# Eight graphs a loop turn, root and scatter one step earlier, and a second home for the last column tile's rows

## What is computed

```python
# layer 0: x = LN(x + D^-1/2 (adj + I) D^-1/2 (x W) + bias)
# layer 1, with h the output of layer 0 and adj the edges' weights:
m_j = h @ W1[:D];  m_i = h @ W1[D:]
pre = m_j[:, None, :, :] + m_i[:, :, None, :] + b1       # [b, i, j, o]
msg = gelu(layernorm(pre, g1, be1))
agg = einsum('bijo,bij->bio', msg, adj)
upd = layernorm(concat([h, agg]) @ W2 + b2, g2, be2)
out = layernorm(h + upd)
```

## Time and profile before

| | us |
|---|---|
| median of 3 runs | 3649.75 (3649.69 to 3650.8) |
| the profiled execution | 3647.8 |
| its span, first to last instruction | 3646.1 |
| PE busy | 3232.9 (89%) |
| ACT busy | 3045.4 (84%) |
| DVE busy | 2937.8 (81%) |
| POOL busy | 2123.0 (58%) |
| DMA, both queues with data | 30% of 16 engines |

### The profile page before, as it was taken

How to read it: one execution, slowest core, us unless ns; L and a number is a source line. 1 busy time by engine, 2 the same in 40 slices (tenths; PEclk the granted TensorE clock), 3 DMA queues, 4 the chain that set the end, 5 groups by cost and what they waited for, 6 DMA issues and landing times.

```text
span 3646.1 us, 88379 instructions
## 1 busy us (share of the span) xinstructions
PE 3232.9 (89%) x26504; PEld 2974.1 (82%) x26505; DVE 2937.8 (81%) x6816; ACT 3045.4 (84%) x8038; POOL 2123.0 (58%) x2628
## 2 busy tenths in 40 slices
PE   4899988989889898889998899988999988989888
PEld 2788888888878888888888888888888888888887
DVE  3788888877878788888788887887887888878887
ACT  3888888988879888888888888888888888988887
POOL 4555666555655556655566655566555666555652
PEclk7999999999989999999999999999999999999999
DMA  2333323223323233332332323333323323223321
GB/s 83 100 95 111 103 94 119 93 86 105 112 80 96 89 102 102 108 110 80 102 103 91 121 78 96 101 105 108 103 87 102 103 92 121 85 89 103 104 91 47
DMA packets 284246, 355.71 MB, mean 98 GB/s; under 512 B 28208, under 2 KB 242736, under 8 KB 283696
## 3 DMA queue, kind: packets, MB, share of 16 engines
q1 hardware_dynamic: 250928, 231.55, 21.7%
q0 software_dynamic: 32768, 117.47, 8.5%
HBM read 223.09 MB, written 125.83 MB: 96 GB/s over the span
## 4 chain that ended last, share of the span: by engine, by line
PE 54%; DVE 17%; ACT 8%; POOL 8%; issue 7%; DMA 5%; DVEq 1%; ACTq 0%; SPq 0%; POOLq 0%; PEldq 0%
PE z_odd_ps L1362 9%; PE agg_odd_ps L1321 9%; PE agg_even_ps L1321 8%; PE z_even_ps L1362 7%; POOL table L512 7%; DMA table<-stage,row_id 5%; DVE pick L1076 4%; PE p_ps L1173 3%; DVE spread L1105 3%; PE z_odd_ps L1358 2%; DVE msg L1051 2%; PE z_even_ps L1358 2%; ACT root L656 2%; DVE stage L940 2%; PE p_ps L1165 2%
## 5 line engine op out<-in xcount | busy, mean ns | idle before, releaser
L711 ACT ACTIVATE tmp<-nbr,r_sb 128x128 f32<-128x128 f32 x4032 | 1262.4, 389 | 25.0
L512 POOL DMA_INDIRECT table<-stage,row_id x512 | 830.3, 1622 | 219.8 <-issue 189.4
L1076 DVE SCALAR_TENSOR_TENSOR pick<-rank,root_p 128x512 f32<-128x512 bf16 (+3 forms) x1536 | 821.3, 564 | 111.3 <-PE z_odd_ps L1362 53.5
L1105 DVE SCALAR_TENSOR_TENSOR spread<-nbr 128x512 f32<-128x512 bf16 (+3 forms) x1536 | 827.5, 564 | 6.9 <-PE agg_even_ps L1321 5.6
L696 ACT ACTIVATE msg<-msg 128x768 f32<-128x768 f32 x768 | 647.2, 843 | 46.2 <-issue 23.5
L1362 PEld LDWEIGHTS z_odd_ps<-mi_g,pick 128*128 128x128 f32 x4608 | 594.4, 200 | 28.8 <-issue 5.0
L1321 PE MATMUL agg_odd_ps<-spread,msg 128*128 128x128 f32 x4608 | 592.5, 280 | 27.3 <-issue 19.6
L1362 PE MATMUL z_odd_ps<-mi_g,pick 128*128 128x129 f32 x4608 | 602.3, 282 | 0.0
L1362 PEld LDWEIGHTS z_even_ps<-mi_g,pick 128*128 128x128 f32 x4608 | 569.1, 193 | 26.8 <-issue 1.9
L527 POOL COPY root_extra<-root_p 128x32 f32<-128x32 f32 (+4 forms) x768 | 276.5, 360 | 530.4 <-ACT root_p L670 530.4
L1321 PEld LDWEIGHTS agg_odd_ps<-spread,msg 128*128 128x128 f32 x4608 | 557.7, 196 | 30.1 <-issue 29.1
(11 more groups left out here) (219 smaller groups left out, 4663.2 us busy)
## 6 DMA issues: line engine op xcount, KB each, us to landing
nbr<-table SPq DMA_DIRECT2D x128, 640.0 KB, 4.8
adj_g<-in_adj SPq DMA_DIRECT2D x32, 1024.0 KB, 7.2
nbr_root<-table SPq DMA_DIRECT2D x128, 256.0 KB, 5.5
nbr_extra<-table SPq DMA_DIRECT2D x384, 70.0 KB
nbr_extra<-table SPq DMA_DIRECT2D x128, 90.0 KB
nbr_extra<-table SPq DMA_DIRECT2D x256, 40.0 KB
x_g<-in_x SPq DMA_DIRECT2D x32, 256.0 KB, 3.4
table<-stage,row_id POOLq DMA_INDIRECT x512, 6.2
```

Source lines behind the costliest of these rows:

```text
L512: pool.indirect_dma_start(table[q], bass.IndirectOffsetOnAxis(ap=row_id[:, jt * TB + it:jt * TB + it + 1], axis=0), stage[:, jt, it, :], N ...
L711: last = act.activation(tmp[:, c % 2, n - FROM[u], :], half_row, ACT.Identity, scale=r_sb[:, c % 2, n - FROM[u]:n - FROM[u] + 1])
L1076: ins = dve.scalar_tensor_tensor(into.rearrange("p k n -> p (k n)"), rank[:, it % 2, span], float(MARK + t), root_p[:, it % 2, span], ALU. ...
L1105: ins = dve.scalar_tensor_tensor(into, ranks(nbr[:, it, jt:jt + count, A_RANK:A_ROOT]), float(MARK + t), nbr[:, it, jt:jt + count, A_ADJ:A ...
```

## The change

`S_ROOT` and `S_SCATTER` go one step back, `S_XB` three steps on; the loop's turn has eight graphs, with four written out ahead of it and four behind; `half` is gone, the root's middle values lie in the rows where the root will stand, and `own` borrows `sqi`; the rows of column tile 3 have a second tensor that every other graph uses.

```diff
+ENDS, TURN_OF = 4, 8
-S_XT, S_DEG, S_XB, S_AT, S_EDGE = 0, 0, 1, 1, 4
+S_XT, S_DEG, S_XB, S_AT, S_EDGE = 0, 0, 4, 1, 4
-S_HB, S_MJ, S_MI, S_SEED, S_ROOT, S_SCATTER, S_OVER, S_OVERS = 18, 17, 21, 17, 19, 20, 22, 23
+S_HB, S_MJ, S_MI, S_SEED, S_ROOT, S_SCATTER, S_OVER, S_OVERS = 18, 17, 21, 17, 18, 19, 22, 23
...
-        half = sb("half", [P, TB, N])
-        stage = sb("stage", [P, TB, TB, ROW])
+        rows_sb = sb("rows_sb", [P, TB, TB, ROW])
+        last_rows = sb("last_rows", [P, TB, ROW])
+        def stage(q, jt):
+            return last_rows[:, :, :] if jt == TB - 1 and q else rows_sb[:, jt, :, :]
+        def halfway(q, jt):
+            return stage(q, jt)[:, :, A_ROOT:ROW]
+        def written(jt, a):
+            return max(a - 1, 0) if jt == TB - 1 and isinstance(a, int) else a - 1 if jt == TB - 1 else a
...
-            with eng.Fori(1, B // 2 - 1) as pair:
-                cx = Pair(eng, pair)
-                for i in range(PC):
+            with eng.Fori(0, (B - 2 * ENDS) // TURN_OF) as turn:
+                cx = Body(eng, ENDS, TURN_OF, turn)
+                for i in range(cx.pc):
                     steps(cx, i)
...
-                        if not is_int(a, 1):
+                        if not is_int(a, 2 if jt == TB - 1 else 1):
                             for it in range(TB):
-                                act.wait_ge(p_scat[jt][it], a * 16)
-                        act.copy(stage[:, jt, :, A_ADJ:A_MJ], p.rearrange("p (i n) -> p i n", i=TB)).then_inc(p_ev, 1)
+                                act.wait_ge(p_scat[jt][it], written(jt, a) * 16)
+                        act.copy(stage(q, jt)[:, :, A_ADJ:A_MJ], p.rearrange("p (i n) -> p i n", i=TB)).then_inc(p_ev, 1)
...
-                        act.activation(half[:, jt, :], root[:, jt, :], ACT.Square).then_inc(p_sq, 1)
+                        if not is_int(a, 2 if jt == TB - 1 else 1):
+                            for it in range(TB):
+                                act.wait_ge(p_scat[jt][it], written(jt, a) * 16)
+                        act.activation(halfway(q, jt), blocks(root[:, jt, :]), ACT.Square).then_inc(p_sq, 1)
...
-                        dve.scalar_tensor_tensor(half[:, jt, :], v, EPS, half[:, jt, :], ALU.add, ALU.mult).then_inc(p_new, 1)
+                        dve.scalar_tensor_tensor(halfway(q, jt), blocks(v), EPS, halfway(q, jt), ALU.add, ALU.mult).then_inc(p_new, 1)
```

More of the change, by code:

```diff
@@ L284, in wait_alone, with __init__ @@
             eng.sem_inc(s_carrier[eng.engine], 1)
[L286 to L294 removed]
+        class Body:
+            def __init__(self, eng, first, graphs, turn=None):
+                self.first = turn is None and first == 0
+                self.last = turn is None and first + graphs == B
+                self.pc, self.blocks = graphs * GC, graphs * TB
+                if turn is None:
+                    self.b, self.units, self.tiles = first, first * GC, first * TB
+                else:
+                    self.b = eng.snap(turn * graphs + first)
+                    self.units, self.tiles = eng.snap(turn * self.pc + first * GC), eng.snap(turn * self.blocks + first * TB)
             def known(self, i):
[L297 removed]
+                return not (self.first and i < 0) and not (self.last and i >= self.pc)
             def prepared(self, i):
                 late = i % GC >= GC - AHEAD
[L302 removed]
+                if i >= self.pc or (self.last and i // GC + 1 + late >= self.pc // GC):
                     return None, 0
@@ L309, in sorted @@
                 if t < SORT_FROM:
-                    return (k, t + UNITS) if i < PC else (None, 0)
-                if i >= PC or (self.last and k + 1 >= 2 * TB):
+                    return (k, t + UNITS) if i < self.pc else (None, 0)
+                if i >= self.pc or (self.last and k + 1 >= self.blocks):
                     return None, 0
@@ L461, in prepare @@
                 if s == S_SUP + 1:
-                    own = half[:, 0, :].rearrange("p (t o) -> p t o", t=TB)
+                    own = sqi[:, :].rearrange("p (t o) -> p t o", t=TB)
                     wait_alone(pool, p_ev, a * NF + (F_SUP + 1))
@@ L547, in steps @@
                 a, s = cx.prepared(i)
-                if i < PC + GC and (a is not None or cx.ended(i) is not None):
+                if i < cx.pc + GC and (a is not None or cx.ended(i) is not None):
                     root_of_x(cx.b + ((i + AHEAD) // GC + 1), (i + AHEAD) % GC)
@@ L713, in steps @@
                 c = i - 4
-                if cx.known(c) and c < PC and where(c)[2] == UNITS - 1:
+                if cx.known(c) and c < cx.pc and where(c)[2] == UNITS - 1:
                     k = c // UNITS
@@ L1056, in steps @@
                 for c in ((0, 1) if cx.first and i == 0 else (i + 1,)):
-                    if c >= PC and (cx.last or c > PC):
+                    if c >= cx.pc and (cx.last or c > cx.pc):
                         continue
@@ L1172, in prepare @@
                         for mt in range(TB):
-                            last = mm(dst, stage[:, mt, it, A_ADJ:A_MJ], sup[:, mt, :], start=(mt == 0), stop=(mt == TB - 1))
+                            last = mm(dst, stage(q, mt)[:, it, A_ADJ:A_MJ], sup[:, mt, :], start=(mt == 0), stop=(mt == TB - 1))
                     if s == S_PROD + 1:
```

53 lines of the change are left out of this document (22 added, 31 removed).

## The result

The changed kernel takes **3542.74 us** (median of 4 runs, 3535.64 to 3546.06), against 3649.72 us before: a ratio of 0.9706, 95% interval 0.9689 to 0.9723. It is 3% faster, 107 us. The forecast was 3505 us, so the sign and the range held and 38 us of the forecast gain did not come.

What follows compares the result with a forecast made beforehand. Bound: the stall in each graph, its end set by POOL's chain. Start 61.4, graph 0 83, 28 graphs at 105.2, graphs 9 and 17 125.3 and 114, turns 7, end 167.3, execution 1.7: 3505 us, range 3430 to 3580.

Steps and rivals of the forecast that it cites:

- The main point: At each graph's stall, POOL's chain sets the end; the change shortens it little: `x_y` only 0.6 to 1.5 us earlier.
- first rival: POOL's scatter run gets shorter, `x_y` ends near 48 and the period is about 103: 3443 us, chance 0.17.
- (c): Sign on POOL: scatters in a group of 4 and one of 12, the last ending 45.4 to 46.4 after the anchor.
- (b): Sign at `dis`: DVE still waits for POOL, 2 to 4 us a graph, `x_y` ending 50.4 to 51.3 after the anchor.
- Part 3: POOL's chain: first scatter at 10.3 instead of 14.4, last done 45.4 to 46.4, `x_y` done 50.4 to 51.3.
- Part 4: Root one step earlier: DVE waits 4.2 us for ACT's square at step 18; loss of 1.1 us, mostly covered at the stall.
- rival at 3564: Late root costs more: PE's gap before step 20's z grows to about 2.6 us, clock falls, period 107.3; chance 0.2.
- Part 5: After the stall: ACT ahead by 2 to 3 us, PE 4 to 5, DVE's step 8 by 3; gain 3 to 5.
- Part 6: Loop turns: 11 fewer at 3.4 us each, or 37 us, goes; no place seen that hides it.
- Part 2: PE's clock after its 4.34 us gap at the stall: at full clock 2.3 us of PE time come back.
- 3533: Rival: ACT's wait for scatters moves to column tile 2, costing 1 us a graph; chance 0.07.
- Part 7: Costed at nothing: wider row stride, four more waits ahead of each L661 on scatters long landed, `own` in `sqi`.

Runs made afterwards that it cites:

- e2: Changed kernel with one home for the rows of column tile 3, always `rows_sb`: 3584.1 us.
- e5: Kernel before the change with two edits only, the second home for column tile 3 and the middle values in the rows: 3575.0 us.
- e3: Changed kernel with the bias add back at step 1, ahead of `x_y` on POOL's queue: 3562.0 us.
- f1: Changed kernel with DVE's multiply by the variance for column tile 0 moved from the head to the end of step 18: 3506.1 us.
- f3: Changed kernel with POOL's two residual operations one step earlier and h plus bias directly behind its copies of the middle values: 3511.8 us.
- e6: Changed kernel with POOL's three residual and bias operations of step 18 on 4 columns instead of 512, output not the reference's: 3509.4 us.
- e7: Changed kernel with POOL's own-row product and its addition to `pre_g` on 4 columns instead of 512, output not the reference's: 3512.8 us.
- e4: Changed kernel with two graphs a loop turn instead of eight, two written out ahead and two behind: 3553.3 us.

## Why the prediction was right, and where it was not

- **The main point held, with less room than was said.** Removing 158 us of waits gave 41 to 70 us (e2, e5), and `x_y` 1.3 us later cost 19 us (e3). But in the changed kernel DVE stands close behind POOL's chain: in f1, f3 and e6 `x_y` ends 5 us earlier and `dis` no earlier. So the first rival's shorter scatter run came in these three, beyond what it had asked for, and its price of 2.2 us a graph did not. Signs (a) and (d) came, (c) with the last scatter 0.3 us ahead of its range, (b) with a shorter wait than the 2 to 4 us said: 1.2 to 1.7 in 16 of 30 graphs and none in eight, since DVE arrives later.
- **Part 3: right in its end, by errors that cancel.** The scatters start at 11.5, not 10.3, because DVE's multiply is late; and they are shorter. From the first to the end of the last are 33.6 us, 5.1 of them extra columns, which leaves 28.5 against 31.4 before. That is the first rival's mechanism in part, spent on the late start. And `x_y` ends 5.9 us behind the scatters, not 4.9: the extra columns between them take 3.9 us instead of 3.2, and `x_y` itself 1.99 instead of 1.68. The 51.0 is in its range by luck.
- **Part 4: the wait of 4.2 us was right, what stands behind it was mis-sized.** "Picks and spreads, 3.3 us" took their lengths from rows where POOL worked mostly on its copies of m_j and not on the residual. They took 4.2 (2632.83 to 2637.05). ACT was 1.6 late at the stall, not 1.1, and PE's gap ahead of step 20's z was 1.73 instead of 1.41, with one of 1.95 ahead of it. That is in part the first half of the rival at 3564; its second half, the fallen clock, did not come (1.00 from 2636 to 2650).
- **Part 5 is the step that failed.** "DVE's step 8 by 3" us ahead became 1.0 (64.4 against 65.4 before). The marks pushed back by `S_XB` were seen for PE, which was in time (60.6); that POOL's next two operations would then stand fully beside DVE's pick and spreads of step 7, which took 2.75 us before and 4.08 now, was not. e7 prices the two operations of POOL at 30 us. f1, f3 and e6 remove it from the other end, since with step 18 in time POOL's row ends earlier and its two operations miss step 7's: 31 to 37 us, nearly all of the miss. e7 leaves step 18 as it is and has 30 of them, so step 7 is the place that counts; with it mended, the late step 18 is worth the few us between at most.
- **Part 6: right in size for the kernel before** (43 us alone, 37 forecast), **wrong in "no place that hides it"**. In the changed kernel the turn seems to meet a DVE that is late anyway (PE waits for it there in e4), and e4 gives 11 us for the part. The two turns that are left were put at 7 us and show 0 and 2.
- **Part 2 and sign (e) held:** the clock went from 0.957 to 0.981 over the span, ordinary graphs at 1.00. Of the rivals, those at 3533 and 3564 us stood nearer to the result than the forecast, but neither mechanism came whole: no wait at tile 2, no fallen clock.
- **Part 7 held.** ACT's totals show no wait for scatters ahead of L682 or L617.

## What to carry to other kernels

When an edit moves one engine's work in time, look up what the other engine of a shared port then runs beside it: lengths read from the old neighbourhood don't hold in the new one. If an instruction has to wait at the head of a queue, put what doesn't need it ahead of it; here that single move gave the 1% by which the change had missed its forecast. Price parts of a change one by one and in both directions, since two of them may remove the same lateness.
